# Per-pair inverse row sums: one VectorE block turn and a DRAM spread in place of widening on GpSimd and turning on TensorE

## What is computed

```python
latent_kv = x @ w_kv_down                       # 256 -> 128
k, v = latent_kv @ w_kv_up                      # 16 heads of 64
q = x @ w_q
att = softmax(where(causal, q @ k.T * 64**-0.5, -inf))
y = (att @ v) @ w_out                           # x = x + gate * y
```

## Time and profile before

| | |
|---|---|
| median of 3 runs | 1807.71 us (1806.67 to 1811.2) |
| profiled execution, first to last instruction (span) | 1806.0 us |
| PE busy | 1747.4 us (97%) |
| DVE busy | 1256.8 us (70%) |
| ACT busy | 890.7 us (49%) |
| POOL busy | 854.1 us (47%) |
| DMA, mean over the span | 91 GB/s |

### The profile page before, as it was taken

The page is one execution under the profiler, slowest core; times in us unless marked ns, Lnnn a source line. Parts: engine busy times, 40 slices in busy tenths (PEclk is TensorE's granted clock), DMA queues, the critical chain, the costliest instruction groups (busy, mean ns, idle before and its releaser), DMA issues.

```text
span 1806.0 us, 40241 instructions
## 1 busy us (share of the span) xinstructions
PE 1747.4 (97%) x15846; PEld 1210.7 (67%) x15846; DVE 1256.8 (70%) x2775; ACT 890.7 (49%) x1970; POOL 854.1 (47%) x1282
## 2 busy tenths in 40 slices
PE   8999999999999999999999999999999999999998
PEld 5666675668566677566856667656685666766667
DVE  5888847626788885753678886675467888576445
ACT  5676624223577763322457675432246767443233
POOL 2777842221187873241138787314114877631420
PEclk9999999999999999999999999999999999999999
DMA  6555570321255554040135555305014555520500
GB/s 185 130 134 125 126 220 14 53 42 38 72 134 133 126 120 143 1 81 14 37 95 132 127 130 132 111 2 94 1 43 109 134 128 122 132 98 2 94 1 26
DMA packets 120188, 164.48 MB, mean 91 GB/s; under 512 B 30305, under 2 KB 87105, under 8 KB 118977
## 3 DMA queue, kind: packets, MB, share of 16 engines
q1 hardware_dynamic: 106032, 155.09, 35.8%
q10 hardware_dynamic: 13968, 6.82, 1.3%
HBM read 63.22 MB, written 4.24 MB: 37 GB/s over the span
## 4 chain that ended last, share of the span: by engine, by line
PE 77%; DVE 10%; ACT 5%; SPq 3%; DMA 2%; issue 1%; POOL 1%; ACTq 0%; DVEq 0%; POOLq 0%
PE bank L680 11%; PE scores L462 11%; PE scores L660 10%; PE bank L462 7%; PE bank L715 4%; SPq L998 3%; DVE prob L809 3%; PE scores L1763 2%; ACT prob L920 2%; PE scores L1673 2%; PE bank L721 2%; PE bank L717 2%; PE scores L1116 2%; PE scores L1735 2%; PE scores L1185 2%; PE scores L433 2%
## 5 line engine op out<-in xcount | busy, mean ns | idle before, releaser
L878 POOL COPY placed<-prob 32x768 f32<-32x768 f32 x384 | 315.5, 822 | 27.5
L291 POOL TENSOR_TENSOR rstd<-rstd,minus_half 128x2 f32<-128x2 f32 x96 | 69.7, 728 | 542.0 <-DVE rstd L290 539.9
L680 PEld LDWEIGHTS bank<-placed,v_t 128*64 128x64 f32 x4608 | 251.6, 137 | 73.9 <-issue 68.3
L680 PE MATMUL bank<-placed,v_t 128*64 128x128 f32 x4608 | 274.4, 276 | 8.1 <-DMA placed<-hx 4.7
L660 PE MATMUL scores<-k_t,q_t 64*128 64x512 f32 (+3 forms) x1536 | 275.1, 496 | 0.8 <-ACT rec_t L930 0.8
L802 DVE CUSTOM_DVE_ANT_0 mod_rows<-scores,hx 128x128 f32<-128x128 f32 (+7 forms) x256 | 191.7, 749 | 75.7 <-PE scores L660 75.7
L809 DVE STREAM_TRANSPOSE prob<-prob 128x1536 f32<-128x1536 f32 x128 | 222.9, 1765 | 27.4 <-ACT prob L920 27.2
L802 DVE CUSTOM_DVE_ANT_0 x<-scores,hx 128x128 f32<-128x128 f32 (+7 forms) x256 | 192.7, 753 | 0.0
L920 ACT ACTIVATE prob<-mod_rows,neg_max 128x128 f32<-128x128 f32 (+2 forms) x192 | 137.4, 716 | 102.9 <-DVE neg_max L802 81.9
L660 PEld LDWEIGHTS scores<-k_t,q_t 64*128 64x128 f32 x1536 | 129.5, 186 | 85.1 <-issue 62.0
L866 POOL COPY rec_wide<-rec 128x128 f32<-128x128 f32 x256 | 64.9, 289 | 226.0 <-DVE rec L813 167.9
(11 more groups left out here) (262 smaller groups left out, 3392.1 us busy)
## 6 DMA issues: line engine op xcount, KB each, us to landing
placed<-prob SPq DMA_DIRECT2D x640, 96.0 KB, 2.2
f<-in_L_ffn_f SPq DMA_DIRECT2D x16, 2048.0 KB, 13.6
placed<-hx SPq DMA_DIRECT2D x320, 96.0 KB, 2.2
mod_rows<-mod_scratch SPq DMA_DIRECT2D x32, 128.0 KB, 4.5
out<-x SPq DMA_DIRECT2D x16, 256.0 KB, 2.1
w_ring<-in_L_attn_w_q ACTq DMA_DIRECT2D x24, 128.0 KB, 2.5
w_ring<-in_L_attn_w_kv_up ACTq DMA_DIRECT2D x48, 64.0 KB, 2.0
next_x<-in_L_attn_x SPq DMA_DIRECT2D x6, 512.0 KB, 4.6
```

Source lines behind the costliest of these rows:

```text
L291: step = pool.do(lambda e, ts=ts: nc.gpsimd.tensor_tensor(rstd[:, ts], rstd[:, ts], minus_half[:, ts], op=ALU.pow), var, filled)
L680: last = nc.tensor.matmul(out_bank[rows_, at_:at_ + P], v_t[pair % 2][:, j, rows_], placed[m % 2][:, :, head, first_block(m, i) + j, :], s ...
L878: nc.gpsimd.tensor_copy(placed[m % 2][target * GROUP:(target + 1) * GROUP, source, :, :, :], prob[m % 3][source * GROUP:(source + 1) * GRO ...
```

## The change

The sums of a pair's 16 rows (2 heads x 8 tiles) are gathered in one block of 16 columns. Once per pair, in its third round, DVE takes the reciprocal of all of them between the two shuffles, and transposes the 128 x 32 block (in 32 x 32 pieces) behind the second. ACT issues the DMA of this block to a scratch in DRAM (two halves, used in turn) at the end of that round, and in the first round of the next pair two DMAs that spread it back, 8 x 128 values to each of the 64 partitions of a head: 256 KB each. POOL's `widen`, PE's `turn_inverse` and ACT's `copy_rec` go, with their waits. `norm` comes four rounds late (`NORM_LAG`), in front of the `keep` of its round, and reads the spread rows. There is one buffer of spread rows, so that the spread of a pair waits for the norms of the pair before. Of the output products, 6 instead of 7 of tiles 0 and 1 stand ahead in the loop.

```diff
+    inverse_dram = nc.dram_tensor("inverse_scratch", [2, 32, P], F32, kind="Internal").ap()
-        rec_t = [part("rec_t", [P, 4 * P]), tmp[:, 0:2, :].rearrange("p t n -> p (t n)")]
-        rec_wide = part("rec_wide", [P, 4, P])
+        inverse_wide = part("inverse_wide", [P, S])
+        inverse, inverse_t = tmp[:, 0, 0:32], tmp[:, 0, 32:64]
+        NORM_LAG = 4
+        BEGUN = PAIRS - 2
...
-            def turn_inverse(m):
-                e.wait_ge(flow["widened"], base["widened"] + m + 1)
...
-                for k in range(len(tiles_in(m))):
-                    last = nc.tensor.transpose(rec_bank[:, k * P:(k + 1) * P], rec_wide[:, k, :], ident[:, :])
-                last.then_inc(flow["rec_turned"], 1)
...
-                for j in range(PAIRS - 1):
+                for j in range(BEGUN):
...
-            def invert(m):
-                k, count = column_of(m, 0, 0), HEADS * len(tiles_in(m))
-                nc.vector.reciprocal(rec[:, k:k + count], row_sum[:, k:k + count]).then_inc(flow["inverted"], 1)
+            def invert(pair):
+                e.wait_ge(flow["exp_done"], base["exp_done"] + PARTS_OF * (pair + 1))
+                nc.vector.reciprocal(inverse[:, 0:HEADS * T], row_sum[:, pair % 2, :]).then_inc(flow["inverted"], 1)
+
+            def turn_inverse(pair):
+                e.wait_ge(flow["inverted"], base["inverted"] + pair + 1)
+                if base["inverse_stored"] + pair:
+                    e.wait_ge(flow["inverse_stored"], base["inverse_stored"] + 16 * pair)
+                nc.vector.transpose(inverse_t, inverse).then_inc(flow["inverse_turned"], 1)
...
-                for head in range(HEADS):
-                    shuffle(m, head)
-                invert(m)
+                shuffle(m, 0)
+                if m % ROUNDS_OF == ROUNDS_OF - 1:
+                    invert(m // ROUNDS_OF)
+                shuffle(m, 1)
+                if m % ROUNDS_OF == ROUNDS_OF - 1:
+                    turn_inverse(m // ROUNDS_OF)
...
             def norm(m):
-                e.wait_ge(flow["kept"], base["kept"] + len(COPIES) * min(m + 2, ROUNDS))
-                e.wait_ge(flow["rec_copied"], base["rec_copied"] + m + 1)
+                pair = m // ROUNDS_OF
+                e.wait_ge(flow["kept"], base["kept"] + len(COPIES) * min(m + NORM_LAG, ROUNDS))
+                e.wait_ge(flow["inverse_spread"], base["inverse_spread"] + 16 * HEADS * (pair + 1))
                 e.wait_ge(flow["values_read"], base["values_read"] + m + 1)
...
             for m in range(ROUNDS):
                 if m > 0:
                     e.wait_ge(flow["kept"], base["kept"] + len(COPIES) * m)
-                widen(m)
+                if m >= NORM_LAG:
+                    norm(m - NORM_LAG)
                 keep(m)
-                if m > 0:
-                    norm(m - 1)
-            norm(ROUNDS - 1)
+            for m in range(ROUNDS - NORM_LAG, ROUNDS):
+                norm(m)
...
+            def store_inverse(pair):
+                e.wait_ge(flow["inverse_turned"], base["inverse_turned"] + pair + 1)
+                e.dma_start(inverse_dram[pair % 2].rearrange("k (a i) -> a k i", a=GROUPS), inverse_t
+                            ).then_inc(flow["inverse_stored"], 16)
+
+            def spread_inverse(pair):
+                e.wait_ge(flow["inverse_stored"], base["inverse_stored"] + 16 * (pair + 1))
+                if pair > 0:
+                    e.wait_ge(flow["normed"], base["normed"] + ROUNDS_OF * pair)
+                for head, rows_ in enumerate(ROWS_OF):
+                    e.dma_start(inverse_wide[rows_, :], inverse_dram[pair % 2, head * T:(head + 1) * T, :].rearrange(
+                        "k i -> (k i)").partition_broadcast(HD0)).then_inc(flow["inverse_spread"], 16)
...
                         exponential(m, i, head)
+                if m > 0 and m % ROUNDS_OF == 0:
+                    spread_inverse(m // ROUNDS_OF - 1)
                 if m in (1, 3):
                     job(*jobs[0])
                 exponential(m, large, 0)
...
-                if m > 0:
-                    copy_rec(m - 1)
+                if m % ROUNDS_OF == ROUNDS_OF - 1:
+                    store_inverse(m // ROUNDS_OF)
             read_values(ROUNDS - 2)
-            copy_rec(ROUNDS - 1)
+            spread_inverse(PAIRS - 1)
             read_values(ROUNDS - 1)
```

More of the change, by code:

```diff
@@ L154, in build @@
     neg_max = sb("neg_max", [P, 16])
[L155 removed]
+    row_sum = sb("row_sum", [P, 2, 16])
     rec = sb("rec", [P, HEADS1])
@@ L589, in out_parts, with out_place @@
             return [(0, 2)] if len(tiles_in(m)) == 2 else [(0, 3), (3, 4)]
-        def out_place(m, lo, hi):
+        def out_place(m, lo, hi, row=None):
             tiles = sorted(tiles_in(m))
             step = tiles[lo + 1] - tiles[lo] if hi - lo > 1 else 1
-            return by_tile(yT[:, m // ROUNDS_OF, :])[:, tiles[lo]:tiles[hi - 1] + 1:step, :]
+            return by_tile(yT[:, m // ROUNDS_OF, :] if row is None else row)[:, tiles[lo]:tiles[hi - 1] + 1:step, :]
+        NORM_LAG = 4
+        BEGUN = PAIRS - 2
         def by_tile(ap):
@@ L762, in pe_pairs @@
                     return [job(0, j) for j in JOBS[:2]]
-                return values(m) if kind == "values" else turn_inverse(m)
+                return values(m)
             for j in JOBS[2:]:
@@ L858, in pool_pairs @@
         def pool_pairs(e):
-            def widen(m):
-                k, count = column_of(m, 0, 0), len(tiles_in(m))
-                e.wait_ge(flow["inverted"], base["inverted"] + m + 1)
-                if m > 0:
-                    e.wait_ge(flow["rec_turned"], base["rec_turned"] + m)
-                for i, tile in enumerate(tiles_in(m)):
-                    at_ = k + HEADS * i
-                    last = nc.gpsimd.tensor_copy(rec_wide[:, out_slot(m, tile), :].rearrange("p (a n) -> p a n", a=HEADS),
-                                                 rec[:, at_:at_ + HEADS].unsqueeze(2).to_broadcast([P, HEADS, HD0]))
-                last.then_inc(flow["widened"], 1)
             def keep(m):
                 e.wait_ge(flow["shuffled"], base["shuffled"] + HEADS * (m + 1))
-                e.wait_ge(flow["widened"], base["widened"] + m + 1)
                 if m > 1:
@@ L913, in exponential @@
             def exponential(m, i, head):
-                k = column_of(m, i, head)
+                k, pair, sum_at = column_of(m, i, head), m // ROUNDS_OF, head * T + tiles_in(m)[i]
+                if m % ROUNDS_OF == 0 and i == 0 and head == 0 and pair > 1:
+                    e.wait_ge(flow["inverted"], base["inverted"] + pair - 1)
                 if i == 0 and head == 0 and b * ROUNDS + m > 2:
@@ L922, in exponential @@
                                      ACT.Exp, scale=-1.0,
-                                     bias=neg_max[:, k:k + 1], accum_out=row_sum[:, k:k + 1]).then_inc(flow["exp_done"], 1)
-            def copy_rec(m):
-                cols = len(tiles_in(m)) * P
-                e.wait_ge(flow["rec_turned"], base["rec_turned"] + m + 1)
-                if m > 1:
-                    e.wait_ge(flow["normed"], base["normed"] + m - 1)
-                nc.scalar.copy(rec_t[m % 2][:, 0:cols], rec_bank[:, 0:cols]).then_inc(flow["rec_copied"], 1)
+                                     bias=neg_max[:, k:k + 1], accum_out=row_sum[:, pair % 2, sum_at:sum_at + 1]).then_inc(flow["exp_done"], 1)
             def read_values(m):
@@ L1099, in batch, with last_products, emit @@
         SPARE_TMP = 2
-        def last_product(ps, t):
-            return lambda e: nc.tensor.matmul(ps, yT[:, PAIRS - 1, t * P:(t + 1) * P], wout[:, PAIRS - 1, :], start=False, stop=True,
-                                              skip_group_check=True)
+        def last_products(ps, t, first):
+            def emit(e):
+                for j in range(first, PAIRS):
+                    last = nc.tensor.matmul(ps, yT[:, j, t * P:(t + 1) * P], wout[:, j, :], start=False, stop=j == PAIRS - 1,
+                                            skip_group_check=True)
+                return last
+            return emit
         def y_ready(t, pair=PAIRS - 1):
```

31 lines of the change are left out of this document (12 added, 19 removed).

## The result

The changed kernel takes **1903.24 us** (median of 4 runs, 1898.93 to 1910.45) where the kernel before took 1807.19 beside it: ratio 1.0529 (95% interval 1.0504 to 1.0554). The prediction had the side right, but 1903 is 55 us above the forecast of 1848 and outside the range of 1822 to 1868.

The account below looks back on a forecast made before the run. PE was taken to bound the loop. Per batch, +11.6 us from holds in the loop, 0 in rounds 0 to 5 and -1.7 in the tail, times 4, gave +40 us: 1848 us, range 1822 to 1868.

Parts of the forecast that it names:

- the side: Whole kernel: the change makes it slower, chance 0.89, against 0.06 for faster and 0.05 for the same.
- The new wait: First round of a pair: ACT waits for POOL's norms until 6.16 us after the shuffles, standing still 2.8 us.
- The sentence on which it hung: DMA waits on ACT's queue: the issuing sequencer waits, so the exponentials behind are held, not only the DMA.
- The issue: ACT's two spread DMAs behind the wait: 0.4 us each to issue, 0.8 with the gap.
- What comes late: Behind ACT's held exponential: DVE's shuffles and PE's second half of q; pairs take 27.1 us, the last pair 26.5.
- Rival 4, PE's clock: Loop: PE idles some 3 us a pair and its clock falls, several tens of us, 1890 or more; chance 0.02.
- Rounds 0 to 5, and the tail: Outside the loop, per batch: rounds 0 to 5 change by 0, the tail after the last shuffle by -1.7 us.
- Rival 1, PE's gain arrives: Spread's wait over when ACT comes: PE's 28 us less some 10 for more waiting, about 1790; chance 0.06.
- Rival 2, gain and holds cancel: Loop: PE's q job and DVE's slack absorb more, a hold of 1 us, not 2.8: about 1806; chance 0.05.
- Rival 3, a slow spread: Spread landing over 10 us also holds the second round's norm and the tail; with 12 us about 1920; chance 0.05.

Follow-up runs that it names:

- e1: Changed kernel with a second place for the spread rows, so a spread no longer waits for the norms of the pair before: 1819.88 us, ratio 1.0070.
- e2: Changed kernel with ACT issuing the spread at the end of a pair's first round; one buffer and the wait stay: 1810.61 us, ratio 1.0014.
- e4: Kernel before with one added wait of ACT for POOL's six copies ahead of the large tile's exponentials, no DMA added: 1846.58 us, ratio 1.0217.
- e3: Changed kernel with 24 unused transposes of the identity on PE before its wait for the second half of q: 1872.0 us, ratio 1.0359.
- e9: From e2, store and spread issued for the first pair of each batch alone, leaving out the other inverses: 1790.47 us, ratio 0.9919.
- e8: From e2, a spread writes 128 of its 1024 columns from each batch's second pair on; issues and waits stay: 1800.58 us, ratio 0.9971.
- e13: Changed kernel with two spread places, later norms, and SyncE issuing stores and the spreads of pairs 0 to 6 behind its moves: 1821.04 us, ratio 1.0090.
- e14: As e13, but ACT issues the spread of the last pair but one at the end of round 21: 1794.11 us, ratio 0.9939.
- e12: Changed kernel with 10 unused transposes of the identity on PE before its wait for the second half of q: 1880.98 us, ratio 1.0404.
- e11: Changed kernel with SyncE's store, two spread places, later norms, and ACT issuing whole spreads at ends of rounds chosen for PE's slack: 1815.92 us, ratio 1.0061.

## Why the prediction was wrong, step by step

The loops lost 90.7 us where the forecast had 46.4. Of the 44.3 between, 33.3 go with PE's clock, which the forecast put at nothing, and 11 are mostly the mis-sized issues.

- **The new wait** (right). Ready at 6.16 predicted, issued at 6.24 measured. e1 and e2 take the hold away and are within 1% of the kernel before. e4, the wait alone, has third rounds 26.8 us apart; the forecast's chain without its issues (27.1 - 0.8), with the 0.66 of transposes that e4 still has on it, gives 27.0. That e4's total of 40 us is also the forecast's is luck: e4 has no issues and no shorter tail. The sentence on which it hung holds: in the changed kernel nothing of ACT runs between 611.68 and the end of the issues at 614.59. The Trainium skill ("DMA: Bandwidth & Descriptors", the anatomy of one DMA) says that the wait is on the issuing sequencer, and this trace agrees. Only ACT's idle time was mis-sized: 1.6 us of waiting and not 2.8, since the store and the weights bring ACT 1.3 us later to the wait.
- **The issue** (mis-sized). I took 0.4 each and said that the time would be higher by this term alone if they took more. They take 0.57 in the median and the two 1.30 with their gap. 0.5 us in 24 holds is 12 us; the loops of e3, in which the clock is held, are 57.3 us longer than before, where the forecast had 46.4: 10.9 more, against 12 by this term. The store costs 0.58 in the median and not 0.4.
- **What comes late** (right). PE's path through the second half of q binds: 27.1 us a pair predicted, 27.5 to 27.8 measured while the clock is up, and for the last pair 26.5 predicted and 26.3 to 26.4 measured in e3.
- **Rival 4, PE's clock** (this is the step that failed). "PE would idle some 3 us in a pair" stood in it, and a price of "several tens of us, 1890 or more", and then a chance of 0.02, because "the clock is 1.00 at 2 us idle in 150". Those rows show only that nothing happens at 2 us in 150; they say nothing of 2.75 us in one gap of 27.8. The forecast itself made the gap, so this was no other case beside it but its next step. It cost 33.3 us in the loops (e3), a good third of the loss there. Without it the loops would have been 10.9 us above the forecast; 46.4 + 10.9 + 33.3 give the loops' 90.7 by construction, as the last two are differences to e3. The price was about right, the chance was not.
- **Rounds 0 to 5, and the tail** (together wrong in sign). From SP's row of round 23 to that of round 5 of the next batch it is 296.5 to 297.2 us, before 295.2: +1.7, where 0 - 1.7 was forecast. Rounds 3 to 5 of the later batches took 24.9 to 26.4 in place of 24.25: probably by the store and the weights ahead of ACT's exponentials, which I had held to cost nothing; no run takes them apart here. The tail has the right sign and half the size. The last `values` of the second batch begin 11.2 us behind SP's row of round 23 (734.16 against 722.99), where 9.9 was predicted and 12.1 stood before; behind the last row of the last batch the execution takes 0.8 us less than before (239.1 and 239.9), not 1.7. The spread was in time: its norms start 11.8 after the shuffles (POOL at 734.82), where the prediction's terms give 11.6.
- **Rival 1, PE's gain arrives** (it did not hold, and its price of 1790 was too good). Its case, a wait that is over when ACT comes, is e1: 1819.88. Even with the inverses for nothing (e9) 28 us are worth 14.8, since PE then waits 16 us more, for moves and q. "Less some 10 us for PE waiting more" was in it.
- **Rival 2, gain and holds cancel** (no). It wanted a hold of 1 us; the large tile's exponential starts 7.6 us after the shuffles in place of 3.3.
- **Rival 3, a slow spread** (no). Landings are 4.0 us in the median, 6.2 at most. Its sum doesn't follow from its words either: 2 us above 10 in each of 28 pairs are 14 a batch, where it has 12.
- **The range.** The forecast's own ends add up to 1828 and 1871, so that the low end of 1826, said to be less than all of them at once, is more; 1903 lies outside by either.

## What to carry to other kernels

A DMA issued from a compute engine's queue holds that engine for as long as its buffer is busy: before you put it there, ask who frees the buffer, and price everything that stands behind. When the forecast makes the bounding engine idle, its clock belongs into the forecast, since the idle gap can be paid twice: here it cost a third of the loss in the loops. And when a spread or copy goes beside transfers that are waited for, its place can decide more than its size: the bytes were worth 8 us (e8 to e2), while e13 and e14, which carry the same bytes and differ in the place and the issuer of one of a batch's eight spreads, lie 27 us apart.

## What the runs showed of the hardware

- PE's clock fell to the 1.2 GHz level in a loop with a gap of 2.75 us in 27.8 (19 stretches in loops with 24 holds); with the gap cut to 0.39 by transposes that nobody reads it hardly did (2 stretches), and the kernel was 31 us faster. In e12 a gap of 1.96 us gave 6 stretches, in e4 one of 1.48 gave 2.
- Two DMA issues on ACT left no gap where they ran beside its exponentials (e1: 0.50 and 0.70 us), and took 1.30 us where ACT was empty behind a wait.
- The 512 KB of a spread, issued by ACT beside the last of SP's moves (603.97 and 604.17 in e11), let the last of these land at 608.27, 4.7 us after the start of its issue, where 2.2 is the median in e9 and in the kernel before.
